# Four heads' values per pass in the first attention, and a later load of the experts' first weights

## The reference, cut to what matters

```
qkv = X @ W_qkv                       # (2, 1024, 16 heads, 64, 3)
q, k, v = (qkv[..., 0], qkv[..., 1], qkv[..., 2])
scores = einsum('bqhd,bkhd->bhqk', q, k) / 8
weights = softmax(scores, axis=-1)
attn = einsum('bhqk,bkhd->bqhd', weights, v)
return attn.reshape(b, s, h * d) @ W_out
```

## Time and profile before

| | us |
|---|---|
| median of 3 runs | 2020.68 (2019.11 to 2021.67) |
| the profiled execution | 2021.03 |
| its span in the trace | 2019.2 |
| PE busy | 1935.5 (96%) |
| DVE busy | 1512.6 (75%) |
| ACT busy | 1384.8 (69%) |
| POOL busy | 1123.5 (56%) |

### The profile page before, as it was taken

One profiled execution on the slowest core, in us unless ns is written; L12 is line 12 of the kernel. 1 busy time (PEld: TensorE's weight loads), 2 busy tenths in 40 slices (PEclk: granted clock), 3 DMA queues, 4 the chain that ended last, 5 costly groups with the idle time before them and its releaser, 6 DMA issues.

```text
span 2019.2 us, 37939 instructions
## 1 busy us (share of the span) xinstructions
PE 1935.5 (96%) x12066; PEld 1664.0 (82%) x12066; DVE 1512.6 (75%) x2595; ACT 1384.8 (69%) x2647; POOL 1123.5 (56%) x1364
## 2 busy tenths in 40 slices
PE   4999999999999999899999899999999999999788
PEld 3888888888888888689999688888888888888666
DVE  5988888888888888753223777777777777777775
ACT  3878787878787878544444677777777777777555
POOL 3655555555555555421000877777777777778522
PEclk9999999999999999999999999999999999999899
DMA  4212111111111111100000000000000000100000
GB/s 114 48 44 48 44 47 43 47 43 47 43 47 43 47 43 46 48 11 4 1 1 1 9 4 9 3 10 0 10 0 10 0 10 0 65 1 1 1 2 20
DMA packets 37767, 51.23 MB, mean 25 GB/s; under 512 B 8489, under 2 KB 17714, under 8 KB 37426
## 3 DMA queue, kind: packets, MB, share of 16 engines
q1 hardware_dynamic: 37682, 50.15, 9.8%
HBM read 15.52 MB, written 1.05 MB: 8 GB/s over the span
## 4 chain that ended last, share of the span: by engine, by line
PE 83%; DVE 6%; issue 4%; ACT 3%; POOL 2%; DMA 0%; SPq 0%; ACTq 0%; DVEq 0%; POOLq 0%
PE ps_t L546 7%; PE ps_o L556 7%; PE ps_t L1018 6%; PE ps_o L557 5%; PE ps_s L578 5%; PE ps_s L579 5%; PE ps_s L1436 5%; PE ps_s L1437 5%; PE ps_s L1438 5%; PE ps_t L1502 3%; PE ps_o L1518 3%; PE ps_o L1520 3%; PE ps_o L1519 3%; PE ps_s L999 2%; PE ps_s L1000 1%
## 5 line engine op out<-in xcount | busy, mean ns | idle before, releaser
L1649 DVE TENSOR_REDUCE a_negmax<-ps_s 128x1 f32<-128x1024 f32 x256 | 312.2, 1220 | 65.2 <-PE ps_s L1438 62.5
L720 DVE TENSOR_REDUCE a_negmax<-ps_s 128x1 f32<-128x1024 f32 x256 | 313.4, 1224 | 53.2 <-PE ps_s L579 38.2
L1573 ACT ACTIVATE a_p<-ps_s,a_negmax 128x1024 f32<-128x1024 f32 x256 | 286.5, 1119 | 93.6 <-DVE a_negmax L1649 92.2
L655 ACT ACTIVATE a_pth<-ps_t 128x512 fp32r<-128x512 f32 x512 | 278.6, 600 | 90.0 <-PE ps_t L546 89.9
L706 DVE TENSOR_TENSOR a_ptl<-ps_t,a_pth 128x512 fp32r<-128x512 f32 x512 | 327.5, 681 | 6.5 <-ACT a_pth L655 5.5
L783 POOL TENSOR_SCALAR a_p<-a_p,a_rsum 128x1024 f32<-128x1024 f32 x256 | 289.5, 1131 | 52.8 <-POOL a_rsum L779 52.8
L1744 POOL TENSOR_TENSOR a_p<-a_p 128x1024 f32<-128x1024 f32 x128 | 307.3, 2400 | 10.7
L779 POOL TENSOR_TENSOR a_rsum<-a_sum,minus_one 128x1 f32<-128x1 f32 x256 | 141.4, 552 | 307.5 <-ACT a_p L685 306.2
L685 ACT ACTIVATE a_p<-ps_s,a_negmax 128x1024 f32<-128x1024 f32 x256 | 288.7, 1128 | 15.3 <-DVE a_negmax L720 15.3
L546 PEld LDWEIGHTS ps_t<-ident_r,a_pr 128*128 128x128 f32 x2048 | 200.4, 140 | 32.0 <-POOL a_p L783 4.0
L556 PE MATMUL ps_o<-a_pth,a_v 128*128 128x512 f32 x512 | 219.9, 430 | 3.9 <-ACT a_o L664 1.3
(11 more groups left out here) (251 smaller groups left out, 4527.3 us busy)
## 6 DMA issues: line engine op xcount, KB each, us to landing
a_q<-a_kh SPq DMA_DIRECT2D x64, 128.0 KB, 2.2
a_q<-a_kl SPq DMA_DIRECT2D x64, 128.0 KB, 2.3
a_kh<-a_kh SPq DMA_DIRECT2D x64, 128.0 KB, 2.2
a_kl<-a_kl SPq DMA_DIRECT2D x64, 128.0 KB, 2.3
a_w_raw<-in_l_w SPq DMA_DIRECT2D x8, 384.0 KB, 3.1
f_raw<-in_ffn_w SPq DMA_DIRECT2D x2, 1408.0 KB, 7.5
f_w_raw<-in_ffn_w SPq DMA_DIRECT2D x9, 256.0 KB, 4.7
f_w<-in_ffn_w SPq DMA_DIRECT2D x9, 256.0 KB, 4.5
```

The lines of the kernel that those rows point to most:

```text
L720: dve.tensor_reduce(a0_negmax[:, s % 4:s % 4 + 1], ps_s[:, s % 2, :, :], AX.XY, ALU.max, negate=True)\
L1649: dve.tensor_reduce(a1_negmax[:, s % 2, m:m + 1], ps_s[:, m, :, :], AX.XY, ALU.max, negate=True)\
```

## The change

- The first attention goes in groups of four heads (`QUAD`), j = 0 to 3. A `v` piece projects 256 tokens for all four heads: six matmuls of 256 columns. There are eight such pieces for four heads, all in the first head (slots 2, 5, 6, 7, 9, 11, 13, 14). Heads 1 to 3 have none; their `qk` and `out` pieces stay where they were.
- ACT and DVE split a `v` piece with two instructions each, since the values of heads 0 and 1 and those of heads 2 and 3 go to two areas of `a0_v`.
- `a0_v` has twice the size. Half of it and the two split value weights lie over `f0_w1_raw`. So `f0_load_early` is no longer issued at the start: SP issues it in the 15th head, behind the copies of the piece of slot 3, after a wait until PE has finished the values of the 14th head.
- PE waits for the splits of values in slots 7 to 10 and 15 of head j = 0 and in slot 0 of j = 1.
- Value weights are loaded for four heads at once (four DMAs), at the start too, and split once in four heads.
- The hardware loop runs over two middle groups of four heads; the first and the last group are emitted apart.

```diff
         A0_PIECES = (
-            {0: ("out", 1), 1: ("qk", 1, 0), 2: ("v", 0, 0), 3: ("qk", 1, 1), 4: ("out", 2), 5: ("v", 0, 1), 8: ("out", 3),
-             9: ("v", 1, 0), 10: ("qk", 0, 0), 12: ("qk", 0, 1), 13: ("v", 1, 1)},
+            {0: ("out", 1), 1: ("qk", 1, 0), 2: ("v", 0, 0), 3: ("qk", 1, 1), 4: ("out", 2), 5: ("v", 0, 1), 6: ("v", 0, 2),
+             7: ("v", 0, 3), 8: ("out", 3), 9: ("v", 1, 0), 10: ("qk", 0, 0), 11: ("v", 1, 1), 12: ("qk", 0, 1),
+             13: ("v", 1, 2), 14: ("v", 1, 3)},
+            {1: ("qk", 1, 0), 3: ("qk", 1, 1), 10: ("qk", 0, 0), 12: ("qk", 0, 1), 13: ("out", 0)},
+            {0: ("out", 1), 1: ("qk", 1, 0), 3: ("qk", 1, 1), 4: ("out", 2), 8: ("out", 3), 10: ("qk", 0, 0),
+             12: ("qk", 0, 1)},
             {1: ("qk", 1, 0), 3: ("qk", 1, 1), 10: ("qk", 0, 0), 12: ("qk", 0, 1), 13: ("out", 0)})
...
-        def a0_pairs(eng, body):
-
-            def pair(p, first, last):
-                for j in range(2):
-                    body(p, j, p * 2 + j, first and j == 0, last and j == 1)
-
-            heads(eng, H0 // 2, pair)
+        def a0_quads(eng, body):
+
+            def quad(p, first, last):
+                for j in range(QUAD):
+                    body(p, j, p * QUAD + j, first and j == 0, last and j == QUAD - 1)
+
+            heads(eng, H0 // QUAD, quad)
...
             if kind == "v":
-                for i in range(TPC):
-                    x = slice(b * SEQ + half * BANK + i * P, b * SEQ + half * BANK + (i + 1) * P)
-                    dst = ps_m[:, i * P:(i + 1) * P]
+                for i in range(2):
+                    x = slice(b * SEQ + (2 * half + i) * P, b * SEQ + (2 * half + i + 1) * P)
+                    dst = ps_m[:, i * QUAD * DH0:(i + 1) * QUAD * DH0]
                     pe.matmul(dst, xT_hi[:, x], a0_wv_hi[:, :], start=True, stop=False)
...
-                        if s in (A0_LAG_PV, A0_LAG_PV + KT):
-                            pe.wait_ge(S["a0_split_lo"], a0_splits(p, j, s - 1, last))
+                        if j == 0 and A0_LAG_PV <= s < A0_LAG_PV + 4 or j == 0 and s == A0_LAG_PV + KT:
+                            pe.wait_ge(S["a0_split_lo"], a0_splits(p, j, s - 2, last))
+                        if j == 1 and s == 0:
+                            pe.wait_ge(S["a0_split_lo"], a0_splits(p, 0, SLOTS - 1, False))
...
-                src = ps_m[:, :].rearrange("p (t j c) -> p t j c", j=2, c=DH0)
-                ins = act.activation(a0_v[b][:, half * TPC:(half + 1) * TPC, :, 0:DH0], src, ACT.Copy)
+                src = ps_m[:, :].rearrange("p (t w j c) -> p w t j c", w=2, j=2, c=DH0)
+                for w in range(2):
+                    ins = act.activation(a0_v[:, w, b, 2 * half:2 * half + 2, :, 0:DH0], src[:, w, :, :, :], ACT.Copy)
...
-                v = a0_v[b][:, half * TPC:(half + 1) * TPC, :, :]
-                ins = dve.tensor_tensor(v[:, :, :, DH0:2 * DH0], src, v[:, :, :, 0:DH0], ALU.subtract)
+                for w in range(2):
+                    v = a0_v[:, w, b, 2 * half:2 * half + 2, :, :]
+                    ins = dve.tensor_tensor(v[:, :, :, DH0:2 * DH0], src[:, w, :, :, :], v[:, :, :, 0:DH0], ALU.subtract)
...
         def a0_load_wv(sp, p):
-            for j in range(2):
-                sp.dma_start(a0_wv_raw[:, j * DH0:(j + 1) * DH0], row(t["l0_wv"], p * 2 + j)[:, 0:DH0])\
+            for j in range(QUAD):
+                at = (j + 2) % QUAD * DH0
+                sp.dma_start(a0_wv_raw[:, at:at + DH0], row(t["l0_wv"], p * QUAD + j)[:, 0:DH0])\
                     .then_inc(S["a0_wv_loaded"], 16)
...
         def f0_load_early(sp):
 
+            sp.wait_ge(S["a0_pv"], 4 * (H0 - 2))
             for e in range(NE):
...
-            f0_load_early(sp)
             f0_load_small(sp)
...
+                    if isinstance(p, int) and p == H0 // QUAD - 1 and j == QUAD - 2 and i == 1:
+                        f0_load_early(sp)
```

More of the change, by code:

```diff
@@ L58, in buffer @@
                     size *= n
-                used[0] += size
+                used[0] += -(-size // 32) * 32
                 return scope.enter_context(nc.sbuf_tensor(name, shape, dt))
@@ L66, in sandwich_kernel @@
         A0_END = 137 * KB
+        QUAD = 4
         A1_KEYS = 109 * KB
@@ L117, in sandwich_kernel @@
         a0_rsum = sb("a0_rsum", [P, 4])
-        sb(None, A0_END)
+        sb(None, A0_END - B * KT * 4 * DH0 * 4)
+        a0_v = sb("a0_v", [P, 2, B, KT, 2, 2 * DH0], F32R)
+        a0_wv_hi = sb("a0_wv_hi", [P, QUAD * DH0], F32R)
+        a0_wv_lo = sb("a0_wv_lo", [P, QUAD * DH0], F32R)
         scope.close()
@@ L473, in sandwich_kernel, with a0_pair @@
         A0_SPLITS = [[s for s in pieces if pieces[s][0] != "out"] for pieces in A0_PIECES]
-        A0_PAIR_SPLITS = len(A0_SPLITS[0]) + len(A0_SPLITS[1])
+        A0_QUAD_SPLITS = sum(len(z) for z in A0_SPLITS)
+        def a0_pair(p, j):
+            return p * 2 + j // 2
         def a0_piece(j, s, first, last):
             piece = A0_PIECES[j].get(s)
-            if piece is None or (first and piece[0] == "out" and j == 0) or (last and j == 1 and s in A0_NEXT):
+            if piece is None or (first and piece[0] == "out" and j == 0) or (last and j == QUAD - 1 and s in A0_NEXT):
                 return None
@@ L483, in a0_splits @@
         def a0_splits(p, j, s, last):
-            n = sum(1 for z in A0_SPLITS[j] if z <= s and not (last and j == 1 and z in A0_NEXT))
-            return p * A0_PAIR_SPLITS + (len(A0_NEXT) + j * len(A0_SPLITS[0]) + n)
+            n = sum(1 for z in A0_SPLITS[j] if z <= s and not (last and j == QUAD - 1 and z in A0_NEXT))
+            return p * A0_QUAD_SPLITS + (len(A0_NEXT) + sum(len(z) for z in A0_SPLITS[:j]) + n)
         def a0_outs(p, j, s):
-            return p * 4 + (3 * j - 3 + sum(1 for z in A0_PIECES[j] if z <= s and A0_PIECES[j][z][0] == "out"))
+            return a0_pair(p, j) * 4 + (3 * (j % 2) - 3 + sum(1 for z in A0_PIECES[j] if z <= s and A0_PIECES[j][z][0] == "out"))
         def a0_bank_free(pe, p, j, s, first, last):
@@ L555, in a0_pe_pv @@
             for kt in range(2 * quarter, 2 * quarter + 2):
-                pe.matmul(ps_o[:, :], a0_v[b][:, kt, j, :], a0_pth[par][:, kt, :], start=kt == 0, stop=False)
-                ins = pe.matmul(ps_o[:, :], a0_v[b][:, kt, j, :], a0_ptl[par][:, kt, :], start=False, stop=kt == KT - 1)
+                pe.matmul(ps_o[:, :], a0_v_of(j, b)[:, kt, :], a0_pth[par][:, kt, :], start=kt == 0, stop=False)
+                ins = pe.matmul(ps_o[:, :], a0_v_of(j, b)[:, kt, :], a0_ptl[par][:, kt, :], start=False, stop=kt == KT - 1)
             if quarter == 3:
@@ L585, in body @@
                             if piece[1] == 0:
-                                pe.wait_ge(S["a0_wo_loaded"], p * 32 + 32)
-                            a0_pe_out(pe, p + (j - 1), piece[1])
+                                pe.wait_ge(S["a0_wo_loaded"], a0_pair(p, j) * 32 + 32)
+                            a0_pe_out(pe, a0_pair(p, j) + (j % 2 - 1), piece[1])
                         else:
@@ L671, in body @@
                         if block >= 0:
-                            o_out(p, j, block)
+                            o_out(a0_pair(p, j), j % 2, block)
                         else:
-                            o_out(p + (j - 1), 1 - j, block + 4)
+                            o_out(a0_pair(p, j) + (j % 2 - 1), 1 - j % 2, block + 4)
                     piece = a0_piece(j, s, first, last)
@@ L686, in body @@
                                    accum_out=a0_sum[:, s % 4:s % 4 + 1]).then_inc(S["a0_exped"], 1)
-            a0_pairs(act, body)
+            a0_quads(act, body)
             g = H0 * SLOTS
@@ L723, in body @@
                     if piece is not None and piece[0] == "out":
-                        add_out((p + (j - 1)) * 4 + piece[1], piece[1])
+                        add_out((a0_pair(p, j) + (j % 2 - 1)) * 4 + piece[1], piece[1])
                     elif piece is not None:
@@ L732, in body @@
                         y0_norm(dve, s - (SLOTS - 3), 0)
-            a0_pairs(dve, body)
+            a0_quads(dve, body)
             g, n = H0 * SLOTS, 2 * H0
@@ L791, in body @@
                         weights(h + 1)
-                    if s == 9 and j == 1 and not last:
-                        pool.wait_ge(S["a0_split_in"], a0_splits(p, 0, 13, False))
+                    if s == 9 and j == QUAD - 1 and not last:
+                        pool.wait_ge(S["a0_split_in"], a0_splits(p, 0, SLOTS - 1, False))
                         value_weights(p + 1)
@@ L842, in body @@
                     sp.dma_start(a0_wqk_raw[:, :], row(t["l0_wqk"], h + 1)).then_inc(S["a0_wqk_loaded"], 16)
-                if j == 1 and not last:
+                if j == QUAD - 1 and not last:
                     sp.wait_ge(S["a0_wv_lo"], p + 1)
@@ L849, in body @@
                     a0_place_qk(sp, h * 4 + (len(A0_NEXT) + i), a0_splits(p, j, s, last), A0_PIECES[j][s])
-                    if j == 0 and i == 2:
```

(10 more changed lines are left out.)

21 lines of the change are left out of this document (10 added, 11 removed).

## The result

The changed kernel takes 2006.27 us (median of 4 runs, 2004.73 to 2006.64) against 2020.52 for the kernel before beside it: a ratio of 0.9928, with a 95% interval of 0.9911 to 0.9946. That is 14.3 us less, where 18.2 less were forecast. The time lies in the range of 1997.5 to 2009. Its profiled execution has a span of 2004.9 us.

A forecast was written before the change was run, and what follows sets the result against it. PE was taken to bound the kernel. Heads -21.1, start +0.9 and loop +2 sum to -18.2 against the profiled 2021.03: 2002.8, or 2002.4 as a median; range 1997.5 to 2009.

The forecast's parts named there:

- Steps 1 and 2: First attention's value pieces: 256-column matmuls at 0.1175 us each make `v` slots about 3.26; the heads sum to -21.1 us.
- rival (c): Value pieces: the 256-column matmul saves nothing, as by the isolated gap; 2023 us, chance 3%.
- Step 3: Splitting values with two instructions on ACT and DVE: costed at 0, bounds 0 and +3 us.
- rival (b): DVE binds the `v` slots, its instructions over chunks of 64 costing more: 12% for 2008 to 2016, 2% for 2017 to 2024.
- Step 4: Handing `ps_m` on between consecutive pieces: PE's added waits for splits and POOL's weight splits cost 0.
- Step 5: Start: two more value-weight DMAs ahead of chunks 1 to 3 of `X` delay DVE's statistics, +0.9 us.
- Steps 6 and 7: 15th head's expert loads, copies ending j = 2: cost 0; at worst up to 5 us once, and 4 x 1.3.
- Step 8: Backward branch between heads 7 and 8 waits for a fetch if the longer body is not held: +2 us, bounds 0 and 6.
- rival (d): Loop, heads 4 to 11, fetched anew each pass, holding PE at its blocks: +40, 2040 us; chance 4%.

The follow-up runs named there:

- narrow kernel: The changed kernel with each values piece again using twelve matmuls of 128 columns in place of six of 256: 2024.39 us, ratio 1.002.
- one-split kernel: The changed kernel with values written as two areas, so ACT and DVE split with one instruction of 512 each: 2005.62 us, ratio 0.9931.

## Why the prediction was right, and where a term was off

From row maximum to row maximum the difference of 14.3 us is made up so (before, after, us):

| stretch | before | after | difference | forecast |
|---|---|---|---|---|
| up to head 0 | 33.34 | 34.23 | +0.9 | +0.9 |
| heads 0 to 3 | 193.1 | 187.7 | -5.4 | -4.6 |
| heads 4 to 14, without the excess in heads 7 and 8 | 560.4 | 544.3 | -16.1 | -16.5 |
| that excess (3.8 + 1.3) | 0 | 5.1 | +5.1 | +2 |
| head 15 to the end of the span | 1232.4 | 1233.6 | +1.2 | 0 |

**Steps 1 and 2, the matmuls and the slots: right.** The forecast for the heads was -21.1; they gave -21.5. `v` slots came out at 3.28 in place of 3.26, since the matmuls stand 0.122 apart and not 0.1175, and j = 0 heads at 55.1 in place of 54.85. The very first head grew by 0.2, not by 0.8: its slot 6 rose to 2.99 as foreseen, but slots 1 and 2 fell from 2.52 and 2.98 to 2.04 and 2.48, which the prediction did not foresee. The narrow kernel shows that the wider matmuls are all of the gain, and it takes rival (c) away: 128-column matmuls that each load weights do cost 0.11 us, not half of it.

**Step 3, the splits: right.** DVE waits in the `v` slots; rival (b) fell with the one-split kernel. **Step 4** too: in heads 4 to 7 PE waits for no split at all, and over the whole attention its waits for splits ahead of a piece are 1.1 us, against 0.8 before.

**Step 5, the start: right**, +0.89, and shown by moving the loads.

**Steps 6 and 7, the moved loads and the copies: right.** The loads end ahead of the copies behind them, and head 7, which begins behind the copies at the end of j = 2, has a first slot of 2.54 with no wait for `a_kh`. That the loads cost nothing was not tried by itself.

**Step 8, the loop: the wait was foreseen and costed too low, and the clock behind it was left out.** I took +2, "one DMA"; it is 5.1. The two kernels whose clock stays up behind the gap put the wait alone at 3.2 to 3.3 us, within the 0 to 6 that the step gives. The other 1.9 are the lower clock, and the prediction has no term for it: its upper end of 6 was three waits for a DMA, so that 5.1 lies below it is partly luck. The trace of the kernel before shows what the lower clock costs, though not that such a gap can bring it on: at its first scores, from 31.82 us on, matmuls of 512 columns are 0.43 us apart, and those from 244.37 in head 4 are 0.23 apart. By the Trainium skill, "Runtime: NRT & Kernel Launch", Instruction fetch mechanics, which gives PE's memory as 2048 instructions, the new body would not fit. The trace agrees, with its 11 loads of q8 in the repetition, and so does the kernel before with a doubled body. Of rival (d) nothing came true: a streamed loop runs at full pace.

**The last stretch** was not in the sum. In the profiled execution of the changed kernel PE's clock drops for a while in the attention's tail, which that of the kernel before does not have:

```profile
811.00:822.00 11.00, 8.75 (x46) 6.92 (x46) 9.90 (x25) 6.43 (x12) 6.88 (x10) 0.84 0.00 0
```

This row is a stretch around the end of head 15 (PE, PEld, DVE, ACT and POOL busy, then the clock, 0.84); the same stretch before, 826.5 to 837.5, has 1.00. But the drop does not account for the difference. The two kernels without it (the kernel before, and PE's loop written out) take 1232.4 and 1232.3 us from head 15 to the end; the ten with it take from 1230.4 to 1234.7. Each is one execution, and executions of one kernel spread by more than that: the kernel before had 2016.7 to 2022.9 in one series of runs. So of the 3.9 us by which I missed, 3.1 are the branch (1.2 its wait, 1.9 the clock), 1.2 this swing, and the heads gave back 0.4. The cause of the swing stays open.

## What to carry to other kernels

Price a matmul from the nearest row with the same shape, with its weight load: here 128 and 256 columns cost 0.11 and 0.12 us, so a pass in half as many matmuls of twice the columns took 0.73 us in place of 1.35. When an edit lengthens the body of a loop, ask whether the engine still holds it: the instruction queue's rows in the repetitions answer that (none there means it is held), and a body that was not held cost 3.2 to 5.8 us at its backward branch here, with PE as the bound, or nothing with PE's loop written out. Ask of such a gap not only how long it is, but what clock the matmuls behind it get. And a piece of work put into a slot that waits for another engine was partly free here: slot 7 grew by 0.54 and slot 11 by 0.43, where an empty slot of 2.55 grew by 0.7.

## What the runs showed of the hardware

- A loop body of about 1300 PE instructions is repeated with no instruction DMA and no gap; one of about 2500 is loaded anew (11 loads of 16 KB in the repetition), and its branch leaves PE without issue for 2.7 to 3.4 us in seven kernels. DVE and POOL wait 1.8 to 2.3 us at theirs, hidden behind PE.
- Instructions that stream for the first time cost nothing visible: heads outside the loop are even 0.1 to 0.2 us shorter than the repeated ones.
- Behind that gap the granted clock fell from 1.00 to 0.50 for 3.3 us or more in five of the seven kernels, and not in the other two. Heads 7 and 8 lost 4.7 to 5.8 us in the five and 3.2 to 3.3 in the two.
